# Set-up of a windowed attention moved into the last expert steps, with loads, small biases and some weighing put elsewhere

## The chip, the cores and the metric

The kernel runs on one core of one Trainium2 chip. A core has TensorE (PE: matrix products and transposes), VectorE (DVE), ScalarE (ACT), GpSimd (POOL) and SyncE (SP, which here only starts transfers). Each engine runs its own list of instructions in order. Engines wait for each other through semaphores. The metric is the device time of one execution in microseconds (us), lower is better. "At" with a number means microseconds from the first instruction of the profiled execution.

## The reference, cut to what matters

There are 4 sequences of 1024 tokens with 128 features. Four sublayers follow each other, and this is the text of the three that the change touches:

```
# 1 linear attention, 16 heads of 8
q = softmax(x @ Wq + bq, features) * s ;  k = softmax(q, tokens) * s
x = x + ga * ((q @ (k.T @ (x @ Wv + bv))) @ Wo + bo)
# 2 experts: 16 of width 64, top 2 of 4 groups, top 4 of the experts left, and a shared one
comb = scores where an expert was chosen, else 0
y = sum_e comb[e] * (silu(x @ w1[e].T) * (x @ w3[e].T)) @ w2[e].T ;  x = x + gb * (y + shared)
# 3 windowed attention, 16 heads of 8, window 64, and the first 16 tokens as a prefix
h = layernorm(x) * (1 + ca) + sa ;  q, k, v = split(h @ w_qkv.T)
x = x + ga * (softmax(q @ k.T over window and prefix) @ v) @ w_out.T
# 4 two layers of local attention and gated feed-forward (not touched)
```

## The kernel before

**Front (at 0 to 284).** One block (`front`, L221) holds sublayers 1 and 2. Sublayer 1 takes 8 chunks of 512 tokens: statistics (`stats`, DVE), root (`rstd`, POOL), normalizing (`apply`, ACT), transpose (PE), scale and shift (`features`, ACT), projections (PE), softmax by `maxima`, `shift`, `sums`, `invert`, `divide` (DVE) and `exp_q`, `exp_k` (ACT). The order in which each engine takes these pieces is written out by hand, one list for each engine. The bias of q is split into three bf16 rows by POOL (`bias_rows`, L372), and six conditioning products (`mods`) come before the first transpose.

**Expert steps (at 81 to 284).** 72 steps in 8 groups of 9: a group is 512 tokens, a step is two of its experts (the first step of a group is the shared expert). Step s runs six products `up` (L602 to L604, PE), `silu` (L814, ACT), `product` (L1066, DVE), `weigh` by the routing weights (L422, POOL; not for the shared expert), and two steps later four products `down` (L622, PE). `up` of step s+2 needs the `product` of step s, and `down` in step s+2 its `weigh`. Four buffers `uu` carry the product.

While these steps run, DVE also routes the next sequence (`lead(s, k)` with k from 11 to 19): `scores`, `groups`, `kept`, four `contest` pieces and `count` (lines L1013 to L1059, with L1026 and L1029 the pairwise comparisons). This falls into steps 3 to 11, 19 to 27 and 37 to 45. POOL also scales the down weights there (`gate_down`, L218, three pieces for each sequence in steps 3, 4, 5 of 18).

**Boundary (at 284 to 306).** `windowed_attention` (L1200) has two blocks. The first loads the weights, normalizes the first tile of all four sequences and makes the prefix keys and values (`kx`, `vpre`, through `hrep`). The second makes queries, keys and values of unit 0 and 1 and then goes through 32 units, tile by tile over the four sequences, four softmax steps each: `scores` (L1533 and L1546, PE), maximum and subtraction (L1402 to L1407, DVE), exponential (L1475, ACT), transposes, weighing. Blocks end with a barrier of all engines.

**Local transformer (at 640 to 1424)**, not touched.

## Time and profile before

| | us |
|---|---|
| median of 3 runs (1425.95 to 1428.6) | 1427.15 |
| the profiled execution | 1425.69 |
| its span, first to last instruction | 1423.9 |
| PE busy / DVE busy | 1278.2 / 1064.5 |
| ACT busy / POOL busy | 869.0 / 740.8 |
| mean granted TensorE clock | 0.964 |

The busy shares are means over stages with different limits, so they don't say what a stage waits for. The stages are told apart by stretches of time, and what ends a wait there is read from the rows of that stretch. POOL's and DVE's rows also show when an instruction of one and the same shape takes longer than elsewhere.

### The profile page before, as it was taken

Reading aid. Unit: us, or ns where it says so; the run is one execution under the profiler, and the core shown is the slowest. Engines: PE = TensorE matmul, PEld = TensorE weight load, DVE = VectorE, ACT = ScalarE, POOL = GpSimd, SP = SyncE. Lnnn points to the kernel's source line nnn. Section 1 sums busy time; section 2 is a strip of 40 time slices with the busy share of each in tenths; the row PEclk is TensorE's granted clock in tenths of the full one; section 3 lists DMA queues with packets and bytes.
Section 4 is the critical chain, followed back from the end, with each engine's and each line's share of the span. In section 5 each row is a group of like instructions: output and inputs, shape, how many; then the busy total and the mean of one; then the engine's idle time right before and its main releaser. Section 6 shows DMA issues by size and latency. Waiting matters only on the chain.

```text
span 1423.9 us, 39853 instructions
## 1 busy us (share of the span) xinstructions
PE 1278.2 (90%) x16225; PEld 992.1 (70%) x16225; DVE 1064.5 (75%) x2355; ACT 869.0 (61%) x2064; POOL 740.8 (52%) x595
## 2 busy tenths in 40 slices
PE   6878899979999999983899999987879999998887
PEld 6767778847777777762688888864557888887554
DVE  6956865348788888874899898855679989898465
ACT  5632222236666666652799989853449999997521
POOL 7345554423343434333877777733247777777010
PEclk9899999959999999995999999999999999999999
DMA  4052354000000000003000101001100000000011
GB/s 147 30 121 54 69 119 103 18 13 3 3 3 3 3 4 3 4 3 97 8 10 9 24 9 33 2 9 31 25 25 12 9 18 16 10 5 9 13 38 47
DMA packets 62038, 41.49 MB, mean 29 GB/s; under 512 B 41233, under 2 KB 51873, under 8 KB 61729
## 3 DMA queue, kind: packets, MB, share of 16 engines
q1 hardware_dynamic: 61280, 38.68, 11.2%
q8 instruction: 130, 2.13, 0.6%
q14 instruction: 52, 0.42, 0.1%
q10 hardware_dynamic: 576, 0.27, 0.1%
HBM read 28.17 MB, written 2.37 MB: 21 GB/s over the span
## 4 chain that ended last, share of the span: by engine, by line
PE 35%; SPq 7%; DVE 5%; POOL 2%; ACT 2%; issue 2%; DMA 1%; DVEq 0%; POOLq 0%; ACTq 0%
SPq L1769 5%; PE PS L2296 4%; PE PS L2282 4%; PE PS L2273 4%; PE PS L2246 4%; PE PS L2316 4%; PE PS L2214 3%; PE PS L2216 3%; PE PS L2215 3%; PE PS L2307 2%; PE PS L2261 2%; PE PS L2385 1%; PE PS L2376 1%; POOL rn L1836 1%; DVE qk L1943 1%
## 5 line engine op out<-in xcount | busy, mean ns | idle before, releaser
L1843 POOL TENSOR_TENSOR rot<-qk,sinl 128x1024 f32<-128x1024 f32 x64 | 218.1, 3408 | 107.7 <-DVE qk L1943 107.7
L1836 POOL TENSOR_TENSOR rn<-ss,neghalf 128x16 f32<-128x16 f32 x64 | 210.3, 3286 | 39.8 <-DVE ss L1936 39.1
L2122 ACT ACTIVATE e_pm<-PS,e_mx 128x128 f32<-128x128 f32 x512 | 151.6, 372 | 18.7 <-DVE e_mx L1927 18.7
L1402 DVE TENSOR_REDUCE d_mx<-PS 128x4 f32<-128x576 f32 x128 | 96.9, 757 | 66.1 <-PE PS L1546 63.2
L422 POOL TENSOR_TENSOR m_work<-m_work,cb 128x512 f32<-128x512 f32 x64 | 83.1, 1300 | 87.3 <-DVE m_work L1066 87.3
L814 ACT ACTIVATE m_work<-PS 128x512 f32<-128x512 f32 x72 | 43.0, 597 | 136.8 <-PE PS L604 136.8
L1465 ACT ACTIVATE pa<-PS 128x512 f32<-128x512 f32 x128 | 76.4, 597 | 61.6 <-PE PS L1555 61.5
L2214 PE MATMUL PS<-wqkv_hi,e_h_hi 128*128 128x512 f32 x192 | 91.3, 475 | 19.5 <-DVE e_h_lo L1920 19.5
L1066 DVE TENSOR_TENSOR m_work<-m_work,PS 128x512 f32<-128x512 f32 x72 | 49.6, 688 | 77.2 <-ACT m_work L814 76.4
L1546 PEld LDWEIGHTS PS<-kx,d_q 32*64 32x64 f32 x2048 | 66.4, 133 | 48.6 <-issue 32.8
L2081 ACT ACTIVATE qk<-PS 128x512 f32<-128x512 f32 x128 | 76.9, 603 | 36.4 <-PE PS L2216 36.3
L1927 DVE TENSOR_REDUCE e_mx<-PS 128x8 f32<-128x1024 f32 x64 | 78.2, 1222 | 27.3 <-PE PS L2273 27.3
L1546 PE MATMUL PS<-kx,d_q 32*64 32x256 f32 (+1 forms) x2048 | 98.0, 306 | 0.0
L1341 POOL TENSOR_TENSOR zvareps<-zmeanvar,epsv 128x1 f32<-128x1 f32 x32 | 6.1, 191 | 174.9 <-DVE zmeanvar L1395 174.9
L2296 PEld LDWEIGHTS PS<-e_vv,e_pa 128*64 128x64 f32 x2048 | 70.0, 137 | 38.0 <-issue 32.2
L2172 ACT ACTIVATE gate<-PS,f_b 128x512 f32<-128x512 f32 x48 | 33.0, 688 | 103.6 <-PE PS L2376 103.6
L2376 PE MATMUL PS<-fT,f_w 128*128 128x512 f32 x192 | 92.5, 615 | 0.0
L2296 PE MATMUL PS<-e_vv,e_pa 128*64 128x65 f32 x2048 | 87.8, 228 | 4.8 <-ACT e_pa L2129 4.8
L1406 DVE TENSOR_TENSOR pm<-PS,d_mx 128x512 f32<-128x512 f32 x128 | 88.5, 692 | 4.4
L1475 ACT ACTIVATE pm<-pm 128x512 f32<-128x512 f32 x128 | 80.7, 631 | 15.1 <-DVE pp L1407 14.6
L1555 PE MATMUL PS<-ident,pm 128*128 128x128 f32 x512 | 80.2, 280 | 7.5 <-ACT pp L1477 7.4
L1943 DVE TENSOR_TENSOR qk<-qk,rn 128x1024 f32<-128x1024 f32 x64 | 78.0, 1218 | 8.4 <-ACT qk L2081 3.4
(272 smaller groups left out, 3613.0 us busy)
## 6 DMA issues: line engine op xcount, KB each, us to landing
cb<-comb_rows SPq DMA_DIRECT2D x32, 512.0 KB, 9.4
zs<-Z SPq DMA_DIRECT2D x64, 32.0 KB
zg<-Z SPq DMA_DIRECT2D x16, 128.0 KB
out_x<-X SPq DMA_DIRECT2D x8, 256.0 KB, 2.6
zs<-Z SPq DMA_DIRECT2D x64, 31.8 KB
zg<-Z SPq DMA_DIRECT2D x16, 127.0 KB
X<-in_L_attn_x SPq DMA_DIRECT2D x3, 512.0 KB, 8.1
wqkv<-in_e_wqkv SPq DMA_DIRECT2D x2, 768.0 KB, 4.4
```

Of the source, the lines that this page charges most:

```text
L422: pool.tensor_tensor(uu[:, s % 4, :], uu[:, s % 4, :], cb[:, g % 2, ORDER[k], :], ALU.mult)\
L1402: chain(dve.tensor_reduce(mx[:, par, :, :], s, AX.X, ALU.max))
L1406: dve.tensor_tensor(out, s[:, :, :, 0:2 * W1], bc(mx[:, par, :, :], 3, 2 * W1), ALU.subtract)
L1475: last = act.activation(p, p, ACT.Exp)
L1546: last = pe.matmul(o, q[r:r + 32, b, rows], kk, start=False, stop=True, skip_group_check=True)
L1836: pool.tensor_tensor(rn[:, v % 2, :], ss[:, v % 2, :], c.neghalf[:, :], ALU.pow).then_inc(rn_ready.sem, 1)
L1843: pool.tensor_tensor(rot[:, :, :, :], x, bc(sinl[:, t, :, :], 2, H2), ALU.mult).then_inc(rot_ready.sem, 1)
L1943: dve.tensor_tensor(x, x, bc(rn[:, v % 2, :], 2, DH2), ALU.mult).then_inc(qk_normed.sem, 1)
L2122: last = act.activation(pm[:, v % 2, h, r, j, :], PS[:, SBANK + r, at * KEYS2:(at + 1) * KEYS2], ACT.Exp, bias=mx[:, v % 2, r, at:at + 1])
L2214: pe.matmul(to, h_hi[:, v % 4, :], w_hi[:, third(k)], start=True, stop=False)
L2296: last = pe.matmul(PS[rows, OBANK + h, at * (DH2 + 1):(at + 1) * (DH2 + 1)], pa[:, h, i, rows], vv[:, b, 4 * h + at, (t + 1 + blk) % 2, :] ...
L2376: last = pe.matmul(PS[:, 2 * (k % 2) + i, :], w1[:, HC * i + j, :], fT[:, g % 2, :], start=True, stop=True)
```

## The change

- `windowed_attention` no longer has blocks of its own. It hands out programs, and `front` runs its set-up (`early(s)`) inside the expert steps 49 to 71 and its 32 units (`main`) right after the last step, in the same block. Before `main`, PE waits for the last product and for the last addition to X.
- The prefix set-up of the four sequences starts in steps 50, 54, 58 and 66, one piece per step (statistics, normalizing, transpose, keys, values), the queries, keys and values of unit 0 and 1 in steps 63 to 70. POOL makes the keys of unit 0 in step 71.
- The tiles of windowed attention exist from the start. Some buffers of the front lie in them, and half of the routing weights lie in Z.
- In routing steps DVE weighs (24 of the 64 weighings). `gate_down` goes from steps 3, 4, 5 of 18 to 13, 14, 15.
- The conditioning weights load in two parts (256 and 512 columns), tokens go ahead of biases and masks in the queue, and the products of the first part come before the first transpose, those of the second behind the first queries. Of the q bias three rows are loaded instead of 128, behind the projection weights, and DVE splits it.
- DVE's first list has `maxima(0)` and `shift(0)` ahead of `stats(3)` to `stats(5)`.

```diff
@@ weigh, on POOL and on DVE
-                    if k in (1, 1 + NJ // 2):
+                    if k and not routed(s):
                         ready = comb_loaded[g % 2][k // (1 + NJ // 2)]
                         pool.wait_ge(ready.sem, ready.at(32 * (g // 2 + 1)))
...
+        def routed(s):
+
+            return any(lead(s, k) for k in range(11, 20))
...
+                    dve.wait_ge(gated.sem, gated.at(s + 1))
+                    dve.tensor_tensor(uu[:, s % 4, :], uu[:, s % 4, :], cb[g % 2][:, ORDER[k], :], ALU.mult)\
+                       .then_inc(u_ready_d.sem, 1)
...
                 for s in range(NS):
                     product(s)
+                    if routed(s) and s % NU:
+                        weigh(s)
@@ POOL
-                    if s // (2 * NU) + 1 < B and s % (2 * NU) in (3, 4, 5):
-                        ex.gate_down(pool, c, s // (2 * NU) + 1, s % (2 * NU) - 3)
+                    if s // (2 * NU) + 1 < B and s % (2 * NU) in (13, 14, 15):
+                        ex.gate_down(pool, c, s // (2 * NU) + 1, s % (2 * NU) - 13)
@@ PE
-                mods(0)
+                mods(0, range(0, 2))
                 turn(0)
-                gate_rows()
                 values(0)
                 turn(1)
                 queries(0)
+                mods(0, range(2, 6))
                 values(1)
                 turn(2)
                 queries(1)
-                mods(1)
+                gate_rows()
                 values(2)
                 context(0)
                 turn(3)
                 queries(2)
                 turn_q(0)
+                mods(1, range(0, 6))
...
+                    early(s)
+                pe.wait_ge(gated.sem, gated.at(NS))
+                pe.wait_ge(added.sem, added.at(NG8))
+                main()
@@ windowed_attention, PE's pieces in the expert steps
+        def early(s):
+            if s in (67, 69):
+                front_t((s - 67) // 2)
+            if s in (68, 70):
+                front_qkv((s - 68) // 2)
+            if at(s, 2) is not None:
+                first_t(at(s, 2))
+            if at(s, 3) is not None:
+                first_k(at(s, 3))
+            if at(s, 5) is not None:
+                first_v(at(s, 5))
```

How the change moves instructions. On PE, before, at the end of the experts: `down` of the last three steps (L622), the barrier, the prefix set-up (L173, L1295, L1300), another barrier, unit 0 and 1 (L1512 to L1521), and the first scores (L1533).

```order
L622 MATMUL PS<-w2g,m_work 128x128 x12
L314 UNCONDITIONAL_BRANCH
L1289 UNCONDITIONAL_BRANCH
L173 MATMUL PS<-ident,xn 128x128 x4
L1295 MATMUL PS<-hT,d_wqkv 128x256 x2
L1300 MATMUL PS<-d_wqkv,hrep 128x128 x4
L1239 UNCONDITIONAL_BRANCH
L1502 UNCONDITIONAL_BRANCH
L1512 MATMUL PS<-ident,xn 128x128
L1519 MATMUL PS<-hT,d_wqkv 128x128
L1520 MATMUL PS<-hT,d_wqkv 128x128
L1521 MATMUL PS<-d_wqkv,hT 128x128
```

On PE, after, the last two expert steps and what follows (L563 to L565 are `up`, L585 `down`, L1559 to L1561 unit 1, L1675 the prefix values of the last sequence, L1577 and L1590 the first scores).

```order
L563 MATMUL PS<-h_hi,w_hi 128x512
L564 MATMUL PS<-h_lo,w_hi 128x512
L565 MATMUL PS<-h_hi,w_lo 128x512
L585 MATMUL PS<-w2g,m_work 128x128 x4
L1675 MATMUL PS<-d_wqkv,hrep 128x128
L585 MATMUL PS<-w2g,m_work 128x128 x8
L1577 MATMUL PS<-mask,identb 128x288 x2
L1590 MATMUL PS<-kx,d_q 64x2x128 x4
```

The two barriers are gone, and the set-up stands one piece at a time behind a `down`.

On DVE, before, two routing steps of the second round (a `product`, L1066, and then one `contest` piece).

```order
L1066 TENSOR_TENSOR m_work<-m_work,PS 128x512
L1026 TENSOR_TENSOR wins<-biased 128x8x11
L1029 TENSOR_TENSOR wins<-biased 128x8x4
L1026 TENSOR_TENSOR wins<-biased 128x8x10
L1029 TENSOR_TENSOR wins<-biased 128x8x5
L1026 TENSOR_TENSOR wins<-biased 128x8x9
```

The same place after (L1052 `product`, L1059 `weigh`, L1012 and L1015 the comparisons).

```order
L1052 TENSOR_TENSOR m_work<-m_work,PS 128x512
L1059 TENSOR_TENSOR m_work<-m_work,cb 128x512
L1012 TENSOR_TENSOR wins<-biased 128x8x11
L1015 TENSOR_TENSOR wins<-biased 128x8x4
L1012 TENSOR_TENSOR wins<-biased 128x8x10
L1015 TENSOR_TENSOR wins<-biased 128x8x5
```

A weighing of 512 columns has come between the product and the comparisons.

On DVE, before, the start behind the first statistics (L917 and L919 `mods`, L923 to L927 `gates`, L933 and L936 `stats`, L941 `maxima(0)`).

```order
L927 TENSOR_TENSOR modT<-modT,gate_sgn 128x2x4
L933 BN_STATS l_stat<-X 128x6 x4
L936 BN_AGGR l_meanvar<-l_stat 128x2 x4
L933 BN_STATS l_stat<-X 128x6 x4
L936 BN_AGGR l_meanvar<-l_stat 128x2 x4
L933 BN_STATS l_stat<-X 128x6 x4
L936 BN_AGGR l_meanvar<-l_stat 128x2 x4
L933 BN_STATS l_stat<-X 128x6 x4
L936 BN_AGGR l_meanvar<-l_stat 128x2 x4
L941 TENSOR_REDUCE mx<-PS 128x64
L947 TENSOR_TENSOR cb<-PS,mx 128x512
```

After, behind the first statistics and one cast (L907 to L913 split the bias, L891 and L893 `mods`, L919 and L922 `stats`, L927 `maxima(0)`; `pa` and `Z` stand for buffers that lie in them).

```order
L907 TENSOR_TENSOR bql<-pa,bqh 96x128
L908 CAST bqh<-bql 96x128
L909 TENSOR_TENSOR bql<-bql,bqh 96x128
L910 CAST bqh<-bql 96x128
L913 COPY bqr<-bqh 32x512 x3
L891 COPY modT<-PS 128x8
L893 TENSOR_SCALAR modT<-modT 128x4
L919 BN_STATS l_stat<-X 128x6 x4
L922 BN_AGGR l_meanvar<-l_stat 128x2 x4
L919 BN_STATS l_stat<-X 128x6 x4
L922 BN_AGGR l_meanvar<-l_stat 128x2 x4
L927 TENSOR_REDUCE mx<-PS 128x64
```

Three `stats` have gone behind `maxima(0)`, and the splitting of the bias has come in front of it.

## Rows read from the trace of the kernel before

**Rows 1.** Timeline of the boundary: start, duration, engine, line, what, [idle before].

```profile
283.06 0.69 DVE L1071 TENSOR_TENSOR X<-X,PS 128x512 f32<-128x512 f32 x1 [2.59 <-PE PS L622]
...
306.22 0.76 DVE L1402 TENSOR_REDUCE d_mx<-PS 128x4 f32<-128x576 f32 x1 [6.88 <-PE PS L1546]
```

**Rows 2.** Timeline: scores of windowed step 4, maxima of steps 4 and 8.

```profile
318.39 0.49 PE L1533 MATMUL PS<-mask,identb 128*128 128x288 bf16 x2
...
319.62 0.76 DVE L1402 TENSOR_REDUCE d_mx<-PS 128x4 f32<-128x576 f32 x1 [2.96 <-PE PS L1546]
...
329.63 0.76 DVE L1402 TENSOR_REDUCE d_mx<-PS 128x4 f32<-128x576 f32 x1 [1.46 <-PE PS L1546]
```

**Rows 3.** Busy of PE, PEld, DVE, ACT, POOL; clock; DMA share and GB/s.

```profile
310.00:315.00 5.00, 5.00 (x73) 3.26 (x72) 1.58 (x4) 2.30 (x6) 0.00 (x0) 0.50 0.01 3
...
320.00:325.00 5.00, 4.91 (x115) 3.30 (x113) 3.96 (x10) 3.28 (x7) 0.73 (x2) 1.00 0.00 0
```

**Rows 4.** Timeline in the expert steps, at full clock: four transposes, four `down`.

```profile
132.76 0.63 PE L562 MATMUL PS<-ident,xn 128*128 128x128 f32 x4 [0.56 <-ACT h_hi L790]
...
134.63 1.05 PE L622 MATMUL PS<-w2g,m_work 128*128 128x128 f32 x8
```

**Rows 5.** Timeline of ACT: `silu` of steps 7, 13, 23, 29, 41, 47, 71.

```profile
106.86 0.60 ACT L814 ACTIVATE m_work<-PS 128x512 f32<-128x512 f32 x1 [1.76 <-PE PS L604]
...
125.23 0.60 ACT L814 ACTIVATE m_work<-PS 128x512 f32<-128x512 f32 x1 [2.74 <-PE PS L604]
...
152.67 0.60 ACT L814 ACTIVATE m_work<-PS 128x512 f32<-128x512 f32 x1 [1.70 <-PE PS L604]
...
172.43 0.60 ACT L814 ACTIVATE m_work<-PS 128x512 f32<-128x512 f32 x1 [3.07 <-PE PS L604]
...
204.59 0.60 ACT L814 ACTIVATE m_work<-PS 128x512 f32<-128x512 f32 x1 [1.70 <-PE PS L604]
...
224.00 0.60 ACT L814 ACTIVATE m_work<-PS 128x512 f32<-128x512 f32 x1 [2.75 <-PE PS L604]
...
279.15 0.60 ACT L814 ACTIVATE m_work<-PS 128x512 f32<-128x512 f32 x1 [1.70 <-PE PS L604]
```

**Rows 6.** Lines on DVE at 56 to 76.4, first routing: busy us, mean ns, idle before.

```profile
L1026 DVE TENSOR_TENSOR wins<-biased 128x120 bf16<-128x120 f32 (+14 forms) x15 | 3.2, 222 | 0.0
...
L961 DVE TENSOR_TENSOR cb<-cb,rs 128x512 f32<-128x512 f32 x2 | 1.4, 692 | 0.1
...
L1051 DVE TENSOR_SCALAR grank<-keep 128x32 f32<-128x32 f32 x1 | 0.2, 182 | 0.0
```

**Rows 7.** Lines on DVE at 196 to 222.6, the routing of the third round.

```profile
L1026 DVE TENSOR_TENSOR wins<-biased 128x120 bf16<-128x120 f32 (+14 forms) x15 | 7.6, 514 | 0.0
...
L1051 DVE TENSOR_SCALAR grank<-keep 128x32 f32<-128x32 f32 x1 | 0.9, 937 | 0.0
```

**Rows 8.** Lines on POOL, at 98 to 223.

```profile
L422 POOL TENSOR_TENSOR m_work<-m_work,cb 128x512 f32<-128x512 f32 x38 | 49.8, 1313 | 54.4 <-DVE m_work L1066 54.4
```

**Rows 9.** DVE's waits at 0 to 23: waited for, us, times, longest.

```profile
DVE ce L910 <- ACT ce L821: 3.2, 1, 3.2
DVE l_stat L933 <- DMA X<-in_L_attn_x: 2.5, 1, 2.5
```

**Rows 10.** All of DVE's waits at 23 to 76.

```profile
DVE rs L953 <- ACT cb L742: 0.2, 1, 0.2
```

**Rows 11.** Timeline of what leads from statistics to `maxima(0)`.

```profile
9.36 0.38 DVE L936 BATCH_NORM_AGGREGATE l_meanvar<-l_stat 128x2 f32<-128x6 f32 x4
...
11.44 0.20 POOL L370 TENSOR_TENSOR l_negmean<-l_negmean,l_rstd 128x4 f32<-128x4 f32 x1
...
13.05 1.64 ACT L720 ACTIVATE cb<-X,l_negmean,l_rstd 128x128 f32<-128x128 f32 x4
...
18.27 0.60 PE L492 MATMUL PS<-ident,cb 128*128 128x128 f32 x4
...
20.02 0.69 DVE L941 TENSOR_REDUCE mx<-PS 128x64 f32<-128x512 f32 x1 [2.30 <-PE PS L512]
```

More of the change, by code:

```diff
@@ L10 @@
+from collections import namedtuple
 from contextlib import ExitStack
@@ L181, with __init__ @@
 class Experts:
-    def __init__(self, c, mc):
+    def __init__(self, c, mc, Z):
         nc = c.nc
@@ L219, in gate_down, with front @@
                            ALU.mult).then_inc(self.w_gated.sem, 1)
-def front(c, A, ex):
+def front(c, A, ex, then):
     nc, X, PS, ident, identb, signal = c.nc, c.X, c.PS, c.ident, c.identb, c.counter
@@ L305, in slot, with by_pool, by_dve @@
             return NC + 2 * r + st
+        def routed(s):
+            return any(lead(s, k) for k in range(11, 20))
+        def by_pool(s):
+            return sum(1 for i in range(s + 1) if i % NU and not routed(i))
+        def by_dve(s):
+            return sum(1 for i in range(s + 1) if i % NU and routed(i))
         def lead(s, k):
@@ L466, in _, with mods @@
             def _(pe):
-                def mods(l):
-                    pe.wait_ge(mod_loaded[l].sem, 16)
-                    for k in range(6):
+                def mods(l, which):
+                    pe.wait_ge(mod_loaded[2 if l == 0 and which[0] else l].sem, 16)
+                    for k in which:
                         last = pe.matmul(PS[:, LB, M0 + (6 * l + k) * B:M0 + (6 * l + k + 1) * B], wmod[l][:, k * D:(k + 1) * D],
@@ L692, in _ @@
                 attend(7)
+                early, main = then.tensor(pe)
                 for s in range(NS + 2):
@@ L885, in _ @@
                 m_apply(1, 1)
+                early, main = then.scalar(act)
                 for s in range(NS):
@@ L902, in _ @@
                         take_comb(lead(s, 22))
+                    early(s)
+                main()
             @block.vector
@@ L1072, in add @@
                                       ALU.add).then_inc(added.sem, 1)
+                dve.memset(bq[0:96, :], 0.0).then_inc(cond_ready.sem, 1)
+                fill, early, main = then.vector(dve, steps, added)
+                fill()
                 dve.memset(c.neghalf[:, :], -0.5)
@@ L1078, in _ @@
                 stats(0)
+                bias_rows()
+                mods(0, range(0, 2), 1)
                 stats(1)
-                mods(0)
-                gates(0)
                 stats(2)
-                stats(3)
-                stats(4)
-                stats(5)
                 maxima(0)
                 shift(0)
+                mods(0, range(2, 6), 2)
+                gates(0)
                 sums(0)
                 invert(0)
+                stats(3)
                 maxima(1)
@@ L1092, in _ @@
                 shift(1)
-                stats(6)
+                stats(4)
+                stats(5)
                 sums(1)
@@ L1096, in _ @@
                 divide(1)
-                mods(1)
+                mods(1, range(0, 6), 3)
                 maxima(2)
@@ L1109, in _ @@
                 residual(0)
+                stats(6)
                 shift(3)
+                sums(3)
                 stats(7)
-                sums(3)
                 m_stats_of(0, 0)
@@ new lines, in ssb @@
+    def ssb(name, shape, dt=F32):
+        return c.sb(name, shape, dt, sc)
+    wqkv = ssb("d_wqkv", [P, 3 * D])
+    wo = ssb("d_wo", [P, D])
+    hmask = ssb("hmask", [P, 4])
+    pmask = ssb("pmask", [P, 8])
+    mask32 = ssb("mask32", [P, 2, KEYS1])
+    mask = ssb("mask", [P, 2, KEYS1], BF16)
+    kx = ssb("kx", [P, B, 4, 3 * W1 + PRE])
+    kraw = ssb("kraw", [P, 2, P])
+    q = ssb("d_q", [P, B, P])
+    vv = ssb("vv", [P, B, H1, 2, VW1])
+    vpre = ssb("vpre", [P, B, 2, 8, VW1])
+    hrep = ssb("hrep", [P, B, 8, PRE])
@@ new lines, in first, with unit, spot, at @@
+    def first(b):
+        return b + 1 if b < 3 else 6
+    def unit(v):
+        return v + 4 if v < 2 else v + 5
+    def spot(b):
+        return b % 2, 1 + b // 2
+    def at(s, k):
+        return START.index(s - k) if s - k in START else None
+    def tile(u):
+        return u // B, u % B
+    def xt(u):
+        return X[:, TB * (u % B) + u // B, :]
+    def sync(sp):
+        for dst, src in ((wqkv[:, :], A["d_wqkvT"]), (wo[:, :], A["d_woutT"]), (hmask[:, :], A["c_hmask"]),
+                         (pmask[:, :], A["c_pmask"]), (mask32[:, :, :], A["c_mask1"])):
+            sp.dma_start(dst, src).then_inc(w_loaded.sem, 16)
```

969 lines of the change are left out of this document (482 added, 487 removed).

## Prediction, made before the changed kernel ran

> **What bounds the kernel now.** I read the stretches of time first, to find stages, then the timeline at the boundary, then per stage the waits and the lines of the engine that waits least. At the boundary nothing is a bound, it is a chain: the last addition of the experts ends at 283.06 + 0.69 = 283.75, and DVE takes the maxima of the first windowed scores at 306.22 [rows 1]. For 22.5 us small pieces wait for each other across engines and two barriers. The reader is to see DVE's idle of 6.88 us in front of the last row, at the end of a stretch that has no work in it longer than about a microsecond.
>
> In the expert steps PE is the bound where nothing is routed: the `silu` rows of steps 47 and 71 stand 55.15 us apart, 2.30 us per step [rows 5]. Where DVE routes, it takes longer: six steps take 18.37, 19.76 and 19.41 us in the three rounds, where six at 2.30 are 13.8 [rows 5]. So the rounds lose 4.6, 6.0 and 5.6 us, together 16.2. (Other slow steps hold PE's own transposes and logits, which stay.) Why DVE is late there, the lines tell: the 15 comparisons L1026 take 3.2 us in the first routing, when POOL weighs nothing, and 7.6 in the third round, and one `grank` takes 182 ns there and 937 here [rows 6, 7]. POOL's weighing of 1313 ns is what runs beside them [rows 8]. A DVE instruction with operands in SBUF stands until POOL's has ended.
>
> In the front, from 23 to 76, DVE waits 0.2 us in all [rows 10]. DVE is the bound there, so its first list is judged by DVE's idle time and DVE's work alone.
>
> **The boundary.** Removed: both barriers and the chain. In its place PE waits for the addition and starts the scores. Added to PE in steps 52 to 71, where PE is the bound: four times a transpose and two products (keys, values), and two times a transpose and three products. A transpose is 0.63 / 4 = 0.16 us, a product of 128 columns 1.05 / 4 = 0.26 [rows 4]: 4 x 0.68 + 2 x 0.94 = 4.6 us. DVE's, ACT's and POOL's pieces lie beside it: in the last steps a step of 2.30 us holds 0.69 of DVE, 0.60 of ACT and 1.3 of POOL. DVE's `early` pieces are a few small ones per step, under a microsecond, POOL's root too. So the addition ends at 283.75 + 4.6 = 288.35. Scores to maxima took 319.62 - 318.39 = 1.2 us at full clock [rows 2], so the first maxima come at 289.6.
>
> Behind that the clock counts. The start ran at 0.50 (310 to 315 is shown) with PE busy all the time, and at 1.00 only from 320 on [rows 3]: steps 0 to 4 took 319.62 - 306.22 = 13.4 us, steps 4 to 8 took 10.0 [rows 1, 2]. In the changed kernel PE comes from steps at full clock with under 1 us of idle, so I take 10.0 for steps 0 to 4: step 4 at 299.6 in place of 319.62. That is -20.0 us, all of it on the path, since from there on the two lists are alike. Bounds: -22 if a part of the PE work falls into PE's idle time; -11 if PE waits at each of its 16 inserted places as it waited for ACT once (0.56, rows 4), 9 us.
>
> What is queued behind the new waits: PE is in order, so an `early` piece whose input is late holds the next `up`. Each piece has its input made one step earlier, but for the transposed unit whose ACT piece shares the step, and `product` may be 1.6 us late before PE notices. POOL makes the keys of unit 0 behind its last weighing, one operation of a size below the weighing's, while PE still does `down` and DVE the addition: hidden. The five loads of windowed attention go behind the others at the start, where they are far from needed. POOL's zeroing and DVE's filling of `vv` (about a microsecond each) fall into the idle time of the start (DVE's 3.2, rows 9).
>
> **The routing steps.** Per round 8 weighings go from POOL to DVE, 24 in all. DVE's weighing has one shape with L961: 692 ns with POOL still [rows 6]; with the wait for the product some 0.79. 8 x 0.79 = 6.3 us more for DVE per round. In turn DVE is no longer held. Over the 14 groups of routing lines the first routing sums to 11.2 us and the third round to 21.8, the second to 20.9 and the first round to 19.2 (rows 6 and 7 show the dearest and one cheap one of each): 8.0, 9.7 and 10.6 us are waits for POOL. `gate_down` was part of them and moves too, to steps where nothing is routed; POOL weighs 1.3 us there and a scaling of 384 columns takes at most 3/4 of that, 2.3 in sum for a step of 2.30: at most 0.3 us. Net for DVE: -1.7, -3.4, -4.3, in sum -9.4. As DVE's lateness goes into the steps one to one, I take -9.4 out of the 16.2. Bounds: -16.2 (all lateness goes, since `up` has slack of its own) and 0 (DVE with two operations in a row before each `down` is late all the same).
>
> The Trainium skill (GPSIMD Engine Reference, Specifications) says that POOL shares its SBUF interfaces with DVE, in contention with DVE instructions "in a 2-port perf mode or with two SBUF inputs". The trace agrees for the comparisons and for `grank` [rows 6, 7]. It speaks against a part of this change: by it the six normalizing instructions put into steps 51 to 67 meet POOL's weighing. Held for a whole weighing they would cost DVE 6 x 1.3 us, still under the 1.6 us of idle time that each step has, so the sum stays.
>
> **The front.** DVE's list, from its idle time. Added work: the split of the bias, five operations on 128 columns and three copies on 512. For the first I take 0.3, between `grank` (0.18, 32 columns) and L961 (0.69, 512 columns), for the copies 0.35, half of L961, since they are bf16 [rows 6]: 2.6 us; it takes the place of a wait for tokens of 2.5 [rows 9], which goes, as POOL's old 4 us do. Then `mods`, and `stats(1)` ends at about 10.4. From the end of the same statistics (9.36 + 0.38 = 9.74) the old chain took 1.9 us to the root [rows 11], ACT 1.65, transposes and queries 20.02 - 18.27 = 1.75: 5.3 us, so `maxima(0)` at 15.7, or at 17 if PE takes nearly twice as long for its part, as at the lower clock. Before it stood at 20.02. But DVE now has done less: three `stats` of 1.25, half of `mods` and the gates are still to do, 5.4 us. With DVE as the bound, DVE stands at 15.7 to 17 + 5.4 - 20.0 - 0.7 (a wait that goes) = 0.4 to 1.7 us later than before. Further, `mods(1)` on PE now stands behind `queries(2)` and `turn_q(0)`, while DVE wants it before `maxima(2)`: by my count DVE waits 2 us there, where it waited for nothing [rows 10]. I take +3. Bounds: +5, and -5 (of DVE's idle time at the start, the 5.7 of rows 9 go and nothing comes in its place).
>
> **Sum.** -20.0 - 9.4 + 3.0 = -26.4 us. Against the profiled execution's own 1425.69 (span 1423.9): 1399.3. The median of the runs is 1.5 above that execution, so I predict 1400.8.
>
> **Rivals.**
> - A: the front gains. For it: fewer bytes ahead, three waits of DVE removed [rows 9]. Against it: what was put behind `maxima(0)` is still DVE's. At -5 in place of +3: 1392.8.
> - B: the routing steps gain nothing. For it: DVE's net is the difference of two large numbers, and the lateness may come from the length of the chain silu, product, weighing and not from DVE's load. Against: DVE shows hardly any idle time there. 1400.8 + 9.4 = 1410.2.
> - C: PE waits at the inserted places, 9 us: 1409.8. For it: the wait of 0.56 for ACT in rows 4 is of that kind. Against: the pieces are spread one per step.
> - D: the clock falls at the new seam, and steps 0 to 4 take 13.4 again: +3.4, 1404.2. In rows 3 PE was busy all of 5 us and still at 0.50. The Trainium skill (TensorE: Matmul & The Clock Gate, What's actually happening) has the gate set by how busy PE has been recently; by it the old idle time is the cause and D does not happen.
> - E, slower: DVE's weighing itself is held or slow, and the waits don't go. Each of the 24 then puts its whole duration into the steps. At 1.3 us, POOL's, they add 31 us and the seam takes back 17: 1427.15 + 14 = 1441. It decides from 0.8 us per weighing with no wait removed. Against it: L961 at 692 ns.
> - That the change does nothing: the branches behind it are written for these very steps, and the order of instructions shows them moved.
>
> **Chances.** Forecast 0.60, A 0.15, B 0.10, C 0.07, D 0.05, E 0.02, others 0.01. The forecast's own range is the bounds of its terms without the far ends, 1395 to 1406. Reaching to A and to B and C: 1391 to 1410. A measurement of this kernel can tell about 0.2%, 2.9 us, from no change. All but E are faster by more: faster 0.97, within 0.2% 0.01, slower 0.02.
>
> **What would show it.** The first maxima of windowed attention about 21 us earlier in relation to the last `silu`, with PE idle under 1 us and the clock at 1.00 in the 15 us behind it. `silu` steps of 2.30 plus 0.2 on average in steps 50 to 71. L1026 at about 3.2 us in each round, L1059 at 0.7 us on DVE, and six routing steps of about 15.5 to 16.5 us. The `silu` of step 7 (106.86 before, rows 5) at about 110, since the front's +3 lies ahead of it. Wrong is the sum if it comes before 105, if the six steps stay at 19, or if PE shows waits for `xn`, `hT` or `hrep` over 3 us in sum.

## The result and the profile after

The changed kernel takes 1406.11 us (median of 4 runs, 1402.31 to 1409.39), the kernel before beside it 1427.88. The ratio is 0.9857, with a 95% interval of 0.9826 to 0.9888: faster by 1.4%. Now and then an execution of any kernel here runs some per cent slower at a lower granted clock; ratios leave these out and medians don't, so a ratio isn't exactly the quotient of two medians. The forecast was 1400.8, with 1395 to 1406 as its own range and 1391 to 1410 as the wide one: the result lies at the upper edge of the first. The profiled execution took 1402.31 us, the lowest of the four (span 1400.5, mean granted clock 0.973), 23.4 less than the profiled one of before.

Where the 23.4 us came from, stage by stage. "Before" and "after" are distances between two rows of one trace (a `silu` start, or the first of the three `d_mx` rows of a scores step):

| stage | before | after | change | forecast |
|---|---|---|---|---|
| start to `silu` of step 0 | 87.89 | 93.05 | +5.2 | +3 |
| three times six routing steps (7 to 13, 23 to 29, 41 to 47) | 57.54 | 47.59 | -9.95 | -9.4 |
| the other steps up to 48 | 80.87 | 80.12 | -0.75 | 0 |
| steps 48 to 71 | 52.85 | 58.75 | +5.9 | +4.6 |
| last `silu` to the first maxima | 27.07 | 5.92 | -21.15 | -21.2 |
| steps 0 to 4 of windowed attention | 13.40 | 12.56 | -0.8 | -3.4 |
| the rest up to the end | | | -1.8 | 0 |

The seam first. Timeline of the kernel after, the last addition (L1065) and the scores behind it (columns: start us, duration, engine, line; in brackets the idle time before and who ended it).

```profile
283.49 0.69 DVE L1065 TENSOR_TENSOR X<-X,PS 128x512 f32<-128x512 f32 x1 [2.25 <-PE PS L585]
284.27 0.41 PE L1577 MATMUL PS<-mask,identb 128*128 128x288 bf16 x2 [0.83 <-DVE X L1065]
...
285.43 0.76 DVE L1373 TENSOR_REDUCE d_mx<-PS 128x4 f32<-128x576 f32 x1 [0.71 <-PE PS L1590]
...
287.35 0.33 PE L1552 MATMUL PS<-ident,xn 128*128 128x128 f32 x1 [0.96 <-DVE xn L1346]
...
290.13 1.12 PE L1599 MATMUL PS<-ident,pm 128*128 128x128 f32 x4 [0.79 <-ACT pp L1504]
```

From the addition's start to the first maxima 1.94 us, where it was 306.22 - 283.06 = 23.16 [rows 1]. The reader is also to see three short waits of PE (0.83, 0.96, 0.79). What they cost stands in the clock. Stretches of the kernel after (columns: us, PE busy, PEld, DVE, ACT, POOL, granted clock, DMA share, GB/s):

```profile
286.00:288.00 2.00, 0.96 (x19) 0.60 (x12) 1.93 (x7) 0.91 (x2) 0.80 (x2) 1.00 0.00 0
288.00:290.00 2.00, 1.34 (x22) 0.85 (x20) 1.77 (x4) 1.52 (x4) 0.55 (x1) 0.84 0.00 0
290.00:292.00 2.00, 1.87 (x38) 1.52 (x39) 0.98 (x3) 0.79 (x4) 0.00 (x0) 0.50 0.03 8
292.00:294.00 2.00, 2.00 (x21) 1.11 (x20) 0.11 (x1) 0.57 (x2) 0.00 (x0) 0.50 0.00 0
294.00:296.00 2.00, 2.00 (x10) 1.85 (x10) 1.47 (x3) 0.56 (x4) 0.00 (x0) 0.50 0.00 0
```

The clock was at its upper level, 2.4 GHz, until about 289 and at 1.2 GHz until 296, although PE had not been idle for as long as a microsecond at once. In [rows 3] it was low at the start of windowed attention too.

The routing stretches, DVE's lines at 201 to 222 (third round; columns: line, busy us, mean ns, idle before). They answer to [rows 7], with L1012 for L1026 and L1037 for L1051:

```profile
L1059 DVE TENSOR_TENSOR m_work<-m_work,cb 128x512 f32<-128x512 f32 x6 | 4.2, 692 | 0.6
...
L1012 DVE TENSOR_TENSOR wins<-biased 128x120 bf16<-128x120 f32 (+14 forms) x15 | 3.3, 223 | 0.0
...
L1037 DVE TENSOR_SCALAR grank<-keep 128x32 f32<-128x32 f32 x1 | 0.2, 183 | 0.0
```

The comparisons take 3.3 us, as good as the 3.2 of [rows 6], and a weighing on DVE takes the 692 ns that the prediction took for it. The `silu` rows of steps 0, 7 and 71, as in [rows 5]:

```profile
93.05 0.60 ACT L783 ACTIVATE m_work<-PS 128x512 f32<-128x512 f32 x1
...
111.86 0.60 ACT L783 ACTIVATE m_work<-PS 128x512 f32<-128x512 f32 x1 [1.70 <-PE PS L565]
...
279.51 0.60 ACT L783 ACTIVATE m_work<-PS 128x512 f32<-128x512 f32 x1 [0.64 <-PE PS L565]
```

In the front, what DVE waits for between 0 and 90 us:

```profile
DVE mx L927 <- PE PS L473: 5.2, 1, 5.2
DVE modT L891 <- PE PS L431: 3.3, 1, 3.3
DVE ce L883 <- ACT ce L791: 2.5, 1, 2.5
```

### The profile page after: what moved, and what is told of

It is laid out like the page before. It is cut to its first block, busy times and chain, and to the rows that moved or that the text cites. A ratio compares the mean times of both kernels' runs of the same rounds, so it can differ in the third digit from the quotient of the medians.

```text
span 1400.5 us, 39911 instructions
## 1 busy us (share of the span) xinstructions
PE 1263.8 (90%) x16229; PEld 986.1 (70%) x16229; DVE 1057.1 (75%) x2389; ACT 869.4 (62%) x2064; POOL 705.2 (50%) x567
## 4 chain that ended last, share of the span: by engine, by line
PE 36%; SPq 7%; DVE 5%; ACT 2%; POOL 2%; issue 2%; DMA 1%; DVEq 0%; POOLq 0%; ACTq 0%
SPq L1852 6%; PE PS L2379 5%; PE PS L2356 4%; PE PS L2365 4%; PE PS L2329 4%; PE PS L2399 4%; PE PS L2297 4%; PE PS L2299 3%; PE PS L2298 3%; PE PS L2390 2%; PE PS L2344 2%; PE PS L2459 1%; PE PS L2468 1%; POOL rn L1919 1%; DVE qk L2026 1%
## 5 line engine op out<-in xcount | busy, mean ns | idle before, releaser
L2205 ACT ACTIVATE e_pm<-PS,e_mx 128x128 f32<-128x128 f32 x512 | 151.6, 372 | 18.7 <-DVE e_mx L2010 18.7
L1492 ACT ACTIVATE pa<-PS 128x512 f32<-128x512 f32 x128 | 76.4, 597 | 60.6 <-PE PS L1599 60.5
L2297 PE MATMUL PS<-wqkv_hi,e_h_hi 128*128 128x512 f32 x192 | 90.6, 472 | 19.7 <-DVE e_h_lo L2003 19.5
L1052 DVE TENSOR_TENSOR m_work<-m_work,PS 128x512 f32<-128x512 f32 x72 | 49.4, 687 | 69.0 <-ACT m_work L783 68.0
L1590 PEld LDWEIGHTS PS<-kx,d_q 32*64 32x64 f32 x2048 | 65.6, 131 | 47.2 <-issue 31.0
L1590 PE MATMUL PS<-kx,d_q 32*64 32x256 f32 (+1 forms) x2048 | 96.3, 302 | 0.0
L2365 PE MATMUL PS<-ident,e_pm 128*128 128x128 f32 x512 | 81.1, 281 | 3.1 <-ACT e_pm L2205 3.0
```

The costliest lines, as they stand in the source:

```text
L1590: last = pe.matmul(o, q[r:r + 32, b, rows], kk, start=False, stop=True, skip_group_check=True)
L2205: last = act.activation(pm[:, v % 2, h, r, j, :], PS[:, SBANK + r, at * KEYS2:(at + 1) * KEYS2], ACT.Exp, bias=mx[:, v % 2, r, at:at + 1])
L2297: pe.matmul(to, h_hi[:, v % 4, :], w_hi[:, third(k)], start=True, stop=False)
L2365: last = pe.transpose(PS[:, TBANK, i * P:(i + 1) * P], pm[:, v % 2, h, i // 2, i % 2, :], ident[:, :])
```

## The experiments

All runs in one table, so that the sections need not repeat it. Times are medians of 4 to 6 runs (one of 10), the ratio is to the kernel before, run on the same chip, with its 95% interval. The stages are those of each run's profiled execution. "Last maxima" is the start of the last row that names `d_mx` in windowed attention (the third row of its last scores step); it was 635.59 before, and 613.89 in the first profile of the changed kernel. The column "silu 0" gives the start of the first `silu`.

| run | us | ratio | silu 0 | steps 0-7 | 3 x 6 routing | 48-71 | to first maxima | steps 0-4 | last maxima |
|---|---|---|---|---|---|---|---|---|---|
| changed, again | 1406.83 | 0.9864 (0.9823-0.9904) | 93.12 | 18.84 | 47.60 | 58.73 | 5.92 | 12.55 | 613.99 |
| weighing on POOL | 1409.12 | 0.9876 (0.9843-0.9909) | 92.67 | 18.68 | 51.80 | 58.73 | 5.91 | 13.52 | 618.97 |
| set-up behind | 1432.12 | 1.0028 (0.9999-1.0057) | 93.87 | 19.36 | 48.06 | 52.86 | 26.93 | 13.93 | 645.65 |
| three statistics ahead | 1410.57 | 0.9862 (0.9820-0.9904) | 91.90 | 22.88 | 47.61 | 58.74 | 5.91 | 14.15 | 624.39 |
| mods(1) ahead | 1405.62 | 0.9835 (0.9805-0.9866) | 93.25 | 19.41 | 47.91 | 58.72 | 5.92 | 12.65 | 615.17 |
| own counts | 1404.56 | 0.9842 (0.9798-0.9886) | 92.84 | 23.35 | 47.55 | 57.07 | 5.92 | 12.56 | 616.52 |
| gate scaling back | 1410.04 | 0.9881 (0.9849-0.9913) | 93.73 | 22.85 | 47.64 | 58.09 | 5.92 | 13.54 | 618.86 |
| fills at the seam | 1400.48 | 0.9821 (0.9796-0.9846) | 93.47 | 18.96 | 47.62 | 58.73 | 6.33 | 9.90 | 612.09 |
| one statistic ahead | 1402.89 | 0.9837 (0.9818-0.9856) | 89.45 | 19.48 | 47.82 | 58.74 | 5.91 | 12.68 | 611.43 |
| fills in step 1 | 1402.48 | 0.9842 (0.9822-0.9862) | 93.60 | 17.39 | 47.61 | 58.74 | 5.91 | 13.51 | 613.83 |
| all together | 1397.04 | 0.9800 (0.9787-0.9814) | 89.53 | 17.40 | 47.59 | 57.08 | 6.33 | 9.90 | 604.90 |

The whole times say little of an edit worth 2 us: the interval of each reaches 0.1 to 0.4% to either side, and what lies behind the last maxima, which no edit touches, took 785 to 791 us in the spans. The runs were also made on three different chips, each beside the kernel before. So each edit is judged by its own stage, and the whole only where it moves by more.

### The changed kernel again

> The changed kernel once more, unedited, so that the edits of it that run beside it have a reference on their own chip. From its first timing: 1406 us, between 1402 and 1410, 0.984 to 0.988 of the kernel before; first silu at 93, last silu at 279.5, last scores maxima of the prefix attention 212.5 us after... that is at about 612.5.

1406.83 us, and every stage within 0.1 us of the first profile, the falls of the clock among them. These are two executions, though: those that were only timed spread from 1402.31 to 1409.39 us in the first run and from 1405.3 to 1415.82 in this one. Where they differ isn't recorded, so it isn't shown that each execution of this program has the same falls of the clock.

### The set-up behind the expert loop

```diff
                 for s in range(NS):
                     ...
-                    early(s)
+                for s in range(NS):
+                    early(s)
                 main()
```

(on PE, ACT, POOL and DVE; on DVE behind the last addition)

> All pieces of the prefix attention's set-up that the changed kernel puts between expert steps 49 and 71 stand in the same order behind the last expert step, still without a barrier. This tells the two halves of the change at the seam apart. Theory (most of the 21 us at the seam is set-up work that now lies beside the expert steps, the barrier itself and the fresh loads are the lesser part): steps 48 to 71 take 52.9 us again instead of 58.8, first scores maxima 18 to 24 us behind the last silu plus 4, so 22 to 26 instead of 5.9, in all 11 to 18 us longer than the changed kernel, 1417 to 1424. Rival (the barriers and the drained engines were the cost, the set-up's instructions pipeline by themselves): first maxima at most 12 us behind the last silu, and with the 5.9 us that the expert steps give back the run is within 2 us of 1406.

For the stages the theory was right: steps 48 to 71 take 52.86 us, what they took before (52.85), and from the last `silu` to the first maxima it is 26.93 us (22 to 26 expected), before with both barriers 27.07. The rival, at most 12 us, is out: the 21 us come from where the set-up lies. What the barriers and the loads are worth, the run doesn't show, as the pieces stand in another order than before. They were not free: PE's first transpose behind the last addition, in the kernel before and in this run:

```profile
288.49 0.66 PE L173 MATMUL PS<-ident,xn 128*128 128x128 f32 x2 [5.46 <-DVE xn L161]
...
282.12 0.48 PE L1666 MATMUL PS<-ident,xn 128*128 128x128 f32 x1 [2.70 <-DVE xn L1394]
```

From the addition's start that is 5.43 us before (283.06 to 288.49, with barrier and loads between) and 2.66 here (279.46 to 282.12). These 2.8 us were lost again behind it, where before the four sequences went through each piece together and here one sequence after the other. Stretches of this run behind the experts:

```profile
276.00:280.00 4.00, 2.39 (x20) 2.01 (x18) 1.23 (x2) 0.08 (x1) 1.26 (x1) 1.00 0.00 0
280.00:284.00 4.00, 1.24 (x3) 0.68 (x3) 1.71 (x8) 0.46 (x1) 0.89 (x3) 0.64 0.00 0
284.00:288.00 4.00, 2.01 (x6) 1.19 (x5) 1.91 (x10) 0.46 (x1) 0.95 (x4) 0.50 0.01 2
288.00:292.00 4.00, 2.29 (x6) 1.50 (x7) 1.68 (x9) 0.46 (x1) 0.37 (x1) 0.50 0.00 0
```

No engine is busy for much over half of any of them (PE's 2.29 is at half the clock): the pieces of four sequences wait for each other in turn. Later in the same run:

```profile
316.00:350.00 34.00, 34.00 (x474) 24.23 (x466) 15.71 (x38) 13.16 (x36) 4.87 (x10) 0.51 0.01 2
```

The clock stayed at its lower level with PE busy for all of 34 us. Steps 4 to 12 of windowed attention took 33.8 us in place of 20.3 in the kernel before, so that in the median the whole gain of the change was gone: 1432.12 us (ratio 1.0028), above the 1417 to 1424 that were expected. Not in every execution: two of the ten took 1419.45 and 1421.94, and their mean clock was 0.963 and 0.961 where the profiled one's was 0.951.

### Weighing on POOL, and the gate scaling back in steps 3 to 5

```diff
-            return any(lead(s, k) for k in range(11, 20))
+            return False
```

> GpSimd weighs the rows in every step, as in the kernel before, VectorE in none; all else as changed. Theory (the three routing stretches were long because GpSimd's weighing held VectorE's routing comparisons): the six steps 7 to 13, 23 to 29 and 41 to 47 take 18.4, 19.8 and 19.4 us again, 10 us more in all than the 47.6 of the changed kernel, and the run is 9 to 11 us longer than it, about 1416. Rival (they became short because the second block of routing, the tokens or the gate's turning are issued in another order): the stretches stay within 2 us of 47.6 and the run within 3 us of 1406.

```diff
-                    if s // (2 * NU) + 1 < B and s % (2 * NU) in (13, 14, 15):
-                        ex.gate_down(pool, c, s // (2 * NU) + 1, s % (2 * NU) - 13)
+                    if s // (2 * NU) + 1 < B and s % (2 * NU) in (3, 4, 5):
+                        ex.gate_down(pool, c, s // (2 * NU) + 1, s % (2 * NU) - 3)
```

> GpSimd scales the gate rows of the next image in steps 3 to 5 of each 18, as in the kernel before, instead of 13 to 15; all else as changed. Theory (these are short and lie beside steps in which VectorE is not late): no stretch changes by more than 0.5 us, time within 2 us of the changed kernel, where TensorE's clock does the same. Rival (they held VectorE in the routing of the next image, whose instructions stand in steps 7 to 13 and 23 to 29): each of the three routing stretches 0.5 to 1 us longer or shorter.

With the kernel before these two make a square (the kernel before also has the old front and the old lists, so its corner differs by more than the two edits). The three routing stretches take, in sum:

| | scaling in 3 to 5 | scaling in 13 to 15 |
|---|---|---|
| POOL weighs | 57.54 (before) | 51.80 |
| DVE weighs | 47.64 | 47.59 (after) |

Moving the weighing is worth 9.9 us where the scaling stands early, and 4.2 where it stands late. Moving the scaling is worth 5.7 us with POOL weighing and nothing with DVE weighing. My first theory for this experiment (10 us) missed: it gave all to the weighing. The stage's forecast of -9.4 holds, since it took both edits together. Why the scaling mattered before, POOL's rows of the kernel before tell, at the second round:

```profile
154.04 1.29 POOL L422 TENSOR_TENSOR m_work<-m_work,cb 128x512 f32<-128x512 f32 x1 [1.49 <-DVE m_work L1066]
155.28 1.04 POOL L218 TENSOR_TENSOR w2g<-w,rowB 128x384 f32<-128x384 f32 x1
157.75 1.30 POOL L422 TENSOR_TENSOR m_work<-m_work,cb 128x512 f32<-128x512 f32 x1 [1.43 <-DVE m_work L1066]
159.00 1.01 POOL L218 TENSOR_TENSOR w2g<-w,rowB 128x384 f32<-128x384 f32 x1
```

and DVE's of the same time:

```profile
154.07 1.38 DVE L1026 TENSOR_TENSOR wins<-biased 128x112 bf16<-128x112 f32 x1
155.38 0.99 DVE L1029 TENSOR_TENSOR wins<-biased 128x8 bf16<-128x8 f32 x1
...
157.78 1.36 DVE L1026 TENSOR_TENSOR wins<-biased 128x80 bf16<-128x80 f32 x1
159.07 1.00 DVE L1029 TENSOR_TENSOR wins<-biased 128x40 bf16<-128x40 f32 x1
```

Each comparison that starts beside one of POOL's operations ends with it. The scalings stood in the list at steps 21 to 23, but behind weighings that waited for DVE, so they ran in the routing steps. With DVE weighing, POOL's list has no such waits there, and with the scaling back in steps 3 to 5 the same three ran together, ahead of the comparisons of that round:

```profile
148.14 2.94 POOL L169 TENSOR_TENSOR w2g<-w,rowB 128x384 f32<-128x384 f32 x3
```

The Trainium skill (SBUF — State Buffer, SBUF: two separate sides) says that an operation of GpSimd that reads SBUF and one of VectorE with two SBUF inputs exclude each other: whichever starts first gets the shared ports for the whole instruction. The rows above of both engines agree, without showing who had the ports: each instruction of DVE ends within 0.12 us of POOL's beside it.

### The counts of first(3) and unit(1)

In the timeline of the kernel after, steps 68 to 71 took 10.30 us for three, where quick ones take 6.9:

```profile
272.97 0.27 PE L1552 MATMUL PS<-ident,xn 128*128 128x128 f32 x1
273.28 0.46 ACT L1510 ACTIVATE hT<-PS,modT 128x128 f32<-128x128 f32 x1 [1.75 <-PE PS L1552]
273.64 0.59 ACT L783 ACTIVATE m_work<-PS 128x512 f32<-128x512 f32 x1
274.11 0.46 ACT L1466 ACTIVATE hT<-PS,modT 128x128 f32<-128x128 f32 x1
...
274.63 0.49 PE L1669 MATMUL PS<-hT,d_wqkv 128*128 128x128 f32 x2 [1.39 <-ACT hT L1466]
```

L1510 is `first_h(3)`. Its own transpose was made at 270.57 (L1662), but it waits for count 6, and the sixth is unit 1's (L1552). The `silu` of step 69 stands behind it in ACT's list. PE's keys of `first(3)` wait for count 6 of `hT` in the same way, which is L1466 of unit 1.

```diff
+    def first_T(b):
+
+        return b + 1 if b < 3 else 5
+
+    def unit_T(v):
+
+        return 4 if v == 0 else v + 5
...
-            act.wait_ge(xnT_ready.sem, xnT_ready.at(first(b)))
+            act.wait_ge(xnT_ready.sem, xnT_ready.at(first_T(b)))
```

(and so at each wait for `xnT_ready` and `hT_ready`)

> The counts at which ScalarE and TensorE wait for the transposed tokens and features of first(3) and unit(1) are set to the order in which TensorE and ScalarE really give them (first(3) fifth, unit(1) sixth); all else as changed. Theory (the slow steps 69 to 71, 10.3 us for three against 7.1 of quick ones, come from ScalarE's wait for a transpose that TensorE makes only at the end of step 69): ScalarE's wait of 1.75 and TensorE's of 1.39 go, steps 69 to 71 take 7.5 to 8.2 us, last silu at 277 to 277.5, and the time is 2.1 to 2.9 us below the changed kernel. Rival (the time is TensorE's own, by the four inserted pieces): the waits go and the steps keep 10 us; or they are gained there and given back at the addition, which then waits for another engine: no change.

Both waits are gone. The three steps take 8.64 us: -1.66, a fifth less than the least that was expected. Part of what is left is a hold, which shows in the timeline of this run:

```profile
272.91 1.28 POOL L380 TENSOR_TENSOR m_work<-m_work,Z 128x512 f32<-128x512 f32 x1
272.98 1.29 DVE L1398 TENSOR_SCALAR xn<-X,meanvar,rstd 128x128 f32<-128x128 f32 x1 [0.35 <-POOL rstd L1315]
```

A normalizing step of 0.34 us is held by a weighing to 1.29. The 1.66 us don't show at the last maxima (616.52 against 613.99): in the profiled execution the clock fell for longer in steps 0 to 7, of which more below. The median is 2.3 us below that of the changed kernel, which is within the noise.

### The front

```diff
                 stats(2)
+                stats(3)
+                stats(4)
+                stats(5)
                 maxima(0)
```

> The statistics of token tiles 3, 4 and 5 stand ahead of maxima(0) on VectorE again, as in the kernel before; all else as changed. Theory (the three statistics of 1.25 us each now stand behind maxima(0), which itself waits 5.25 us for TensorE in the trace after, and VectorE is what the rest of the front waits for): the wait shrinks to 1.5 us, maxima(0) still begins at about 17, the first silu comes 3.7 us earlier, at 89.3, and the run is 3.7 us shorter than the changed kernel, 1402. Rival (the front's end is set by the weight loads or by TensorE's modulations, and VectorE is not late): first silu within 1 us of 93, time within 1 us of the changed kernel.

1.2 us in place of 3.7, and theory and rival both missed. `maxima(0)` came at 17.47 as expected, but POOL was done early with its deviations, went on to split weights, and held the small gate operations of DVE, as the timeline of this run shows:

```profile
19.83 2.75 POOL L163 TENSOR_TENSOR w_lo<-m_work,w_hi 128x576 fp32r<-128x576 f32 x2
19.92 1.33 DVE L899 TENSOR_TENSOR modT<-modT,gate_sgn 128x8 f32<-128x8 f32 x1
...
21.29 1.33 DVE L900 TENSOR_SCALAR modT<-modT 128x8 f32<-128x8 f32 x1
```

Unheld they take 0.17 each. The two held ones add 2.3 us, nearly the 2.5 that are missing. The last maxima came even 10.4 us later than in the changed kernel, by the clock, as shown below.

```diff
                 gate_rows()
+                mods(1, range(0, 6))
                 values(2)
                 context(0)
...
                 turn_q(0)
-                mods(1, range(0, 6))
                 context(1)
```

> TensorE multiplies the second half of the modulations, mods(1), directly behind the gate's rows, ahead of values(2), as in the kernel before; all else as changed. Theory (VectorE's wait of 3.32 us for these products at 32.4 is on the path): the wait goes and the first silu comes 2.5 to 3.3 us earlier, time 1403. Rival (what is ahead of it takes its place: values(2) and the context behind it come later by the time of mods(1), so VectorE waits there instead): first silu within 0.8 us of 93, and a new wait of VectorE of 2 to 3 us between 20 and 32.

The rival was right: `silu` 0 at 93.25, and DVE's longest wait for `mx` is 5.9 us in place of 5.2, its sum 7.7 over four. So the wait of 3.32 for `mods(1)` was only the last in a chain, and the trace after shows its head:

```profile
22.31 0.23 POOL L338 TENSOR_SCALAR l_negmean<-l_meanvar 128x4 f32<-128x4 f32 x1 [7.96 <-DVE l_meanvar L922]
...
24.13 1.65 ACT L689 ACTIVATE Z<-X,l_negmean,l_rstd 128x128 f32<-128x128 f32 x4 [3.51 <-POOL l_negmean L341]
...
25.68 0.61 ACT L717 ACTIVATE Z<-Z 128x512 f32<-128x512 f32 x1
...
26.35 0.88 PE L491 MATMUL PS<-v,Z 128*128 128x129 f32 x3 [3.24 <-ACT Z L717]
```

POOL waits for `stats(3)`, ACT's `apply(3)` for POOL, and behind it in ACT's list stands `exp_k(0)`, for which PE's `context(0)` waits with all its list. Hence only `stats(3)` ahead:

```diff
                 stats(2)
+                stats(3)
                 maxima(0)
...
                 invert(0)
-                stats(3)
                 maxima(1)
```

> Only the statistics of tile group 3 stand ahead of maxima(0) on VectorE, those of 4 and 5 stay behind it; all else as changed. Theory (in the changed kernel ScalarE's apply(3) waits 3.51 us until 24.13 for the deviation that GpSimd works out from these statistics, and exp_k(0), on which TensorE's context(0) waits at 26.35, is queued behind it; with all three ahead GpSimd went on to split weights at 18.6 to 22.5 and held four small operations of VectorE, which ate the gain): apply(3) waits less than 0.5 us, context(0) begins at 22.5 to 24, no small operation of VectorE at 18 to 20 takes over 0.3 us, and the first silu comes at 90 to 91, 2 to 3 us earlier than the 93.1 of the changed kernel. Rival (the front behind 40 us waits for something else): context(0) early, first silu within 1 us of 93.1.

The theory holds, with more than it promised; ACT in this run:

```profile
21.11 1.64 ACT L689 ACTIVATE Z<-X,l_negmean,l_rstd 128x128 f32<-128x128 f32 x4
22.98 0.63 ACT L717 ACTIVATE Z<-Z 128x512 f32<-128x512 f32 x1 [0.24 <-DVE Z L947]
```

`context(0)` begins at 23.67, and the first `silu` comes at 89.45, 3.7 us earlier. One statistic behind `maxima(0)` was 3.7 of the 5.2 us that the front had lost.

### TensorE's clock

At the seam PE was given products to make in its three waits:

```diff
+        def fill(n):
+            for _ in range(n):
+                pe.matmul(PS[:, UBANK, 0:2 * KEYS1], identb[:, :], bc(mask[:, 0, :], 1, 2), start=True, stop=True)
...
+                    if k == 0:
+                        fill(3)
                     scores(k)
+                    if k in (1, 2):
+                        fill(4)
```

> TensorE multiplies the mask 11 times more (of 0.2 us each at the full clock, into a bank that nobody reads before it is overwritten) where it waits at the seam: 3 ahead of scores(0), 4 behind scores(1), 4 behind scores(2). All else as changed. Theory (the granted clock fell to 0.50 at 289.3 us, four steps into the prefix attention, because TensorE had been busy only some two thirds of the 9 us before): the clock stays at 1.00 through the seam, the first maxima of steps 0 to 4 take about 10 us instead of 12.56, the fills themselves cost 0 to 0.5, and the last maxima of the prefix attention come 2 to 2.5 us earlier: 1404. Rival (the fall hangs on something else, such as what the experts did long before): the clock falls at the same place, the steps take 12.6 to 13.2 us, and the time is 0 to 1 us longer.

The same stretches as above, in this run:

```profile
286.00:288.00 2.00, 1.92 (x34) 1.08 (x26) 1.61 (x4) 0.00 (x0) 1.12 (x2) 1.00 0.00 0
288.00:290.00 2.00, 1.64 (x15) 1.08 (x19) 1.93 (x6) 1.68 (x3) 0.73 (x2) 1.00 0.00 0
290.00:292.00 2.00, 1.81 (x50) 1.24 (x45) 1.73 (x5) 1.08 (x3) 0.00 (x0) 1.00 0.03 8
292.00:294.00 2.00, 2.00 (x50) 1.57 (x39) 0.71 (x1) 1.03 (x3) 0.00 (x0) 1.00 0.00 0
```

The clock stays at 1.00. Steps 0 to 4 take 9.90 us, 2.65 less, the fills cost 0.41 ahead of the first maxima, and this is the 10.0 that the prediction took for these steps. The last maxima come 1.9 us earlier (2 to 2.5 expected). The run's median is 6 us below the changed kernel's, on another chip; what goes beyond the 1.9 lies where nothing was edited.

The second place is the wait of 5.2 us between `up` of steps 1 and 2:

```diff
+                    if s == 1:
+                        pe.wait_ge(ctx_scaled.sem, ctx_scaled.at(B))
+                        for _ in range(18):
+                            pe.matmul(PS[:, YB, :], ex.w1_hi[:, 0:P], h_hi[:, tok(0)], start=True, stop=True)
                     if s < 2:
                         turn_x(1, s)
```

> TensorE makes 18 products of 128x512 more (0.24 us each at the full clock, into a bank that nobody reads before it is overwritten) in its 5.2 us of waiting between expert steps 1 and 2, at 89.9 to 95.2; all else as changed. Theory (the fall of the granted clock to 0.50 at 94 to 96, which lasted 3.4 us in the changed kernel and 13.7 in three of its variants and made their steps 0 to 7 take 18.8 or 22.9 to 23.4 us, follows this idle stretch): no fall between 90 and 110, steps 0 to 7 in 17 to 18.2 us, time 1 us below the changed kernel and never 4 above. Rival (the fall comes whatever TensorE does there): 18.8 or about 23 again.

Two stretches of the run with its own counts, without fills:

```profile
94.00:96.00 2.00, 1.07 (x5) 1.11 (x6) 0.85 (x2) 1.27 (x3) 1.14 (x1) 0.50 0.53 111
...
104.00:106.00 2.00, 2.00 (x6) 1.57 (x5) 0.00 (x0) 0.00 (x0) 0.00 (x0) 0.50 1.08 226
```

The same stretches of the run with fills in step 1:

```profile
94.00:96.00 2.00, 0.98 (x6) 0.54 (x5) 0.69 (x1) 2.00 (x4) 0.39 (x1) 1.00 0.79 167
...
104.00:106.00 2.00, 2.00 (x15) 1.77 (x14) 1.74 (x5) 0.60 (x1) 0.00 (x0) 1.00 1.07 226
```

Steps 0 to 7 take 17.39 us, the least of all runs. Without the fills they took 18.7 to 19.5 in seven programs and 22.9 to 23.4 in three (three statistics, own counts, scaling back), where the clock stayed at 0.50 until about 106 or 107. The wait before the fall was 5.2 us in all ten; the low stretch behind it lasted 3.4 us in four, 6.8 in three and 13.7 in these three. Two of the three differ from the changed kernel by edits outside these steps. The third puts POOL's scaling into steps 3 to 5, but the kernel before has it there too and took 18.97. The moment of the first `silu` doesn't sort them either (92.84 with the long stretch, 92.67 with a short one). What decides how long the clock stays low is open; that may differ from one execution to the next of the same program, since each of the three was profiled once and their timed executions spread over 9 us and more.

For the profiled executions the clock accounts for what the last maxima show: with own counts 4.5 us lost in steps 0 to 7; with the three statistics 4.0 lost there and 7.6 more behind the first maxima, where the clock was low for 27 us.

### All together

> All mends together: statistics of group 3 ahead of maxima(0), the waits of first(3) and unit(1) at the counts in which they are really given, the 11 fills at the seam and the 18 between expert steps 1 and 2. If the terms add (first silu -2.5, steps 0 to 7 -1, late steps -1.7, seam -2.3): 7.5 us below the changed kernel, 1399, and 0.98 of the kernel before; last maxima of the prefix attention at 606 to 607 instead of 614.0. Rival (mends of the front and of the clock eat one another, because a shifted program meets other clock stretches): 1402 to 1404.

The terms add: first `silu` -3.6, steps 0 to 7 -1.4, late steps -1.65, seam -2.2, in sum -8.9, and the last maxima come at 604.90, 9.1 us earlier than in the changed kernel. 1397.04 us, ratio 0.9800 (0.9787 to 0.9814) to the kernel before. This is the fastest version: 9 us below the changed kernel, whose ratio's interval (0.9826 to 0.9888) it doesn't touch.

## Why the prediction was right, point by point

- **The boundary** (-16.6 up to the first maxima): right, and for its reason. Measured +5.9 - 21.15 = -15.3. The addition to first maxima was taken as 1.2 us from the addition's end, and is 1.25 (283.49 + 0.69 to 285.43). The prediction didn't split the gain between the barriers and the place of the set-up; by the run with the set-up behind the loop nothing is gained without the place, though 2.8 us of barrier and loads went.
- **PE's added work** (+4.6): +5.9, mis-sized by 1.3. The sentence that failed is "Each piece has its input made one step earlier, but for the transposed unit whose ACT piece shares the step". Two waits were for a count that another piece gives, and gone with the own counts (-1.66, which leaves +4.2).
- **The ramp** (-3.4, measured -0.8: "PE comes from steps at full clock with under 1 us of idle, so I take 10.0"): this is the step that failed. PE's idle stretches were under 1 us, as foreseen, and the clock fell nevertheless: 12.56 us. This is rival D, which had been given 0.05 with +3.4 us; it came with +2.6. With the fills the 10.0 is there. The sentence by the Trainium skill (TensorE: Matmul & The Clock Gate, What's actually happening) was read as "no fall": that the gate follows how busy PE has been agrees with the fills, but the old idle time was not the only cause. With PE's recent work alone it is also hard to explain why the clock stayed low through 34 us of busy PE in the run with the set-up behind.
- **The routing steps** (-9.4): -9.95, each round within 0.6 us of its own term (-1.7, -3.4, -4.3 against -2.25, -3.45, -4.25). Taking both edits in one sum was what saved it: the prediction didn't know that either edit alone would have gained more than half. "At most 0.3 us" for the scaling in its new place was right: the steps from 7 to 48 outside the routing took 61.31 us with it and 61.25 with the scaling back.
- **The front** (+3): +5.2, outside its bound of +5. `maxima(0)` at 17.13 (15.7 to 17 forecast) and the split of 2.3 us (6.83 to 9.12, 2.6 forecast) came nearly as computed. The failing step is "With DVE as the bound": from `stats(3)` behind `maxima(0)` a chain through POOL, ACT and PE ran, and DVE waited for its end (3.3 us, where 2 were forecast for `mods(1)`). The single statistic ahead gives 3.7 us back. The remaining 1.5 is not settled; the wait for `ce` ends 0.93 us later than before (5.11 against 4.18).
- **Rival A** (front -5) and **B** (routing nothing) were both wrong; **C** (9 us at sixteen places) came at two places, with 1.4 us for `hT` and 0.4 for `xn`, so the sign of being wrong (over 3 us of such waits) didn't come; **E** is excluded by 692 ns per weighing.

The sum was 4.7 us too good for the stages up to the last maxima (-26.4 against -21.7), and 1.7 us more were gained behind them, where nothing was forecast. That part is luck: the second profile of the same kernel took 2.9 us longer behind the last maxima than the first. By the medians the gain is 21.8 us against a forecast of 26.4, so the forecast time was right in its terms for the seam and the routing and 5 us too low by the ramp, the front and PE's added work.

## What to carry to other kernels

The set-up gained here by lying beside other work; taking the barriers away alone gained nothing. Before a piece is moved, the chain that it heads is followed through every engine's list, since one statistic of 1.25 us here cost 3.7. Two edits against the same lateness don't add, so both corners are tried. Edits of a few microseconds are judged by the stage that they touch, with the granted clock beside it, since the clock's low stretch behind one and the same wait was worth 4 us more or less from one run to another.

## What was not expected of the hardware

- The granted clock fell to 0.50 at 289, behind waits of 0.83, 0.96 and 0.79 us with work between them, and stayed there for some 7 us with PE busy nearly throughout. It fell there in all 8 programs with the set-up in the expert steps and no fills at the seam, and in neither of the 2 with them. In the 8 it stayed low for about 7 us in four, 10 in three and 27 in one.
- With the set-up behind the loop the clock was low (0.51) through 34 us in which PE was busy all the time. What brings it back up isn't shown by any run.
- In steps 0 to 7, the length of the low stretch behind one wait of 5.2 us was 3 to 7 us in seven programs and 13.7 in three, and the same in the two profiles of the changed kernel.
- An operation of DVE with 8 columns (0.17 us) and one normalizing 128 (0.34) took 1.33 and 1.29 beside POOL's operations: how long they were held followed POOL's operation and not their own size.
